# Statistics of a second new batch per group on ScalarE, with a tile of its own for what its passes write

## The chip, the cores and the metric

The kernel runs on one core of a Trainium2 chip. The metric is the device time of one execution in microseconds (us), the median of several runs. The engines are named as in the profile: PE (TensorE), DVE (VectorE), ACT (ScalarE), POOL (GpSimd) and SP (SyncE, which here only issues DMAs).

## The reference

Input `x` is 32 batches of 256 x 1024 (S x N, float32), `adj` is 256 x 256 and serves as the weight of both layers; `b1` and `b2` have 256 elements.

```python
h = jnp.maximum(_layernorm(x, axis=-1), 0.0)      # mean and variance over the 1024 columns of each row
x = x + gnn(h, adj, b1, adj, b2)

def gnn(x, W1, b1, W2, b2):                        # x: (32, 256, 1024)
    adj = construct_adj(x, 8)                      # from the column means: top-9 nodes of an outer product
    xr = jnp.swapaxes(x, 1, 2)
    h = jax.nn.relu(gc(xr, adj, W1, b1))
    h = gc(h, adj, W2, b2)
    return jnp.swapaxes(h, 1, 2)
def gc(x, adj, W, b):                              # degree-normalised adjacency after a linear layer
    return jnp.einsum('bij,bjh->bih', adj / deg, x @ W.T + b)
```

The graph is an outer product of one vector with itself, so its nodes fall into a few classes. The kernel computes the linear layers in full and replaces the product with the 1024 x 1024 graph by sums per class.

## The kernel before

The 32 batches go in 8 groups of 4 (`FIRST[g]` is the first batch of group g). A batch lies in SBUF as 128 partitions x 2 chunks x 1024 columns. 12 slots (`NX`) hold raw batches, 10 slots (`NHL`) the layer-normalised ones, each split in a high and a low float16 part. For each batch:

- Statistics. Either DVE makes them: four `bn_stats` of 128 x 512 (`stats`, L1032 to L1041) and two `bn_aggr` (`mean_var`, L1043); or ACT makes them (`scalar_stats`, L585): a sum pass over each chunk (L594), two small scalings, a square pass over each chunk (L601) and two more small scalings. `on_scalar` (L329) says which: batches 10 and 11, and from 12 on the last batch of each group.
- ACT takes the square root of the variance (`root`, L572), DVE its reciprocal (`root_inverse`, L1051, which counts up `r0_ready`), and POOL makes scale and bias from it in seven small operations (`coefs`, L802 to L820, which begins with a wait for `r0_ready` and ends by counting up `coef_ready`).
- ACT applies them with a relu (`h_chunk`, L614) and writes the high part (`h_hi`, L623); DVE writes the low part (`h_lo`, L1062).
- PE does layer 1 as units of 12 matmuls of 128 x 512 (L430) and adds the graph's part with small matmuls (`rows`, L441). ACT and DVE evict it as a new high and low part (`y_hi` L635, `y_lo` L1071); PE does layer 2 on those, and DVE adds it to `x` (`final`, L1087).

Between these lie the chains of a group. DVE searches the column means for the top nodes (`top_a` to `top_e`, `kinds`) and writes the class mask `onehot[:, g % 2]` (`classes`, L1133). POOL gathers columns of the top nodes (`gather`, L834), DVE sums them (`top_sums`, L1160), and POOL makes the first-layer class input of it (`plain_q1`, L846 and L848). PE multiplies that by the weights (`plain_rows`, L474 with q1r), DVE, ACT, DVE, ACT and DVE turn the result into rows (`rows_x`, `round_rows`, `rows_t`, `round_rest`, `rows_w`). `class_sizes` (L468), `class_q1` (L863 on), `times_q1` (L494) and, for layer 2, `times_q2` (L474 with q) follow the same pattern.

Each engine works through an order written out by hand; a wait holds up everything behind it on its engine. In round g of the main loop (from g = 1) the statistics are those of batches `FIRST[g] + 8` to `FIRST[g] + 11`, and there are such batches in rounds 1 to 5. The orders that matter, in round g:

- POOL (L1006 on): `coefs(first+8)`, `class_sums`, `u_nodes`, `put_u`, `coefs(first+9)`, `late_sums(g)`, the four `gather` of group g+1, **`coefs(first+10)`, `plain_q1(g+1)`, `coefs(first+11)`, `class_q1(g+1)`**.
- ACT (L773 on): `split_rows(2g+1)`, in round 1 the two `make_h` of batch 13, `root(first+10)`, `scalar_stats(first+11)`, `root(first+11)`, `make_h(front(g,3), 0)` (this is batch first+10), `class_count(g+1)`, `split_rows(2g+2)`, `make_h(front(g,3), 1)`, the two of batch first+11.
- DVE (L1433 on): as the loop at L1365 shows.
- PE (L519 on): layer 1 of group g, then layer 2; `plain_rows(g+1)` comes behind `rows(*us[4:6])` of layer 2, then two units, `class_sizes(g+1)` and `rows(*us[6:])`.

What ACT's statistics passes write is not used. It goes into the mask tile `onehot[:, (g + 1) % 2]`, the one that `classes(g+1)` writes next. For that reason `scalar_stats` waits for `l2_ps` (the last readers of that tile) and `classes` for `act_sums` (L1128).

Of the kernel before, what the change touches and what calls it, by code (L numbers as in the profile page):

```python
# [100 lines left out]
def gnn_kernel(nc, x, adj_t, bias1, bias1_row, bias2_row, consts, out):  # L101
# [3 lines left out]
    with ExitStack() as ctx:  # L105
        def sb(name, shape, dt=F32):
            return ctx.enter_context(nc.sbuf_tensor(name, shape, dt))
# [31 lines left out]
        cr = sb("cr", [P, 96], F16)  # L139

        bn = sb("bn", [P, 2, KC, 2, 6])
        mv = sb("mv", [P, RB, KC, 2])
        sums = sb("sums", [P, 2, KC])
        minus = sb("minus", [P, KC])
# [118 lines left out]
        def ends(g):  # L263

            if g < 0:
                return 0
            return FIRST[g] + SIZES[g] if g < NG else B
# [60 lines left out]

        def on_scalar(n):  # L329

            return n in (NX - 2, NX - 1) or n >= NX and n == ends(GROUP[n]) - 1

        def on_scalar_in(g):

            return sum(on_scalar(n) for n in range(min(FIRST[g] + NX, B)))

        def by_vector(n):

# [226 lines left out]
        def _(act):  # L565
# [16 lines left out]
            def scalar_count(n):  # L582
                return n + 1 - by_vector(n)

            def scalar_stats(g, n):  # L585

                if not is_batch(n):
                    return
                done_before, junk = scalar_count(n) - 1, onehot[:, (g + 1) % 2]
                for k in range(KC):  # L590
                    act.wait_ge(x_in[n % NX][k], 16 * (n // NX + 1))
                    if g > 0 and k == 0:
                        act.wait_ge(l2_ps, NH * ends(g - 1))
                    act.activation(junk, xs[:, n % NX, k], ACT.Copy, accum_out=sums[:, 0, k:k + 1]  # L594
                                   ).then_inc(act_sums, 1)
                    act.wait_ge(act_sums, 2 * KC * done_before + k + 1)
                act.activation(mv[:, n % RB, :, 0], sums[:, 0], ACT.Copy, scale=1.0 / N).then_inc(act_means, 1)
                act.activation(minus[:], sums[:, 0], ACT.Copy, scale=-1.0 / N).then_inc(act_means, 1)
                act.wait_ge(act_means, 2 * (done_before + 1))
                for k in range(KC):  # L600
                    act.activation(junk, xs[:, n % NX, k], ACT.Square, bias=minus[:, k:k + 1],  # L601
                                   accum_out=sums[:, 1, k:k + 1]).then_inc(act_sums, 1)
                    act.wait_ge(act_sums, 2 * KC * done_before + KC + k + 1)
                for k in range(KC):
                    act.activation(mv[:, n % RB, k, 1:2], sums[:, 1, k:k + 1], ACT.Copy, scale=1.0 / N
                                   ).then_inc(act_vars, 1)
# [57 lines left out]
            def make_h(n, k):  # L664
                if n is not None:
                    h_chunk(n, k)
                    h_hi(n, k)
# [45 lines left out]
            root(9)  # L713
            means_copy(1, 1)
            make_h(8, 1)
            scalar_stats(0, 10)
            root(10)
            scalar_stats(0, 11)
            root(11)
            make_h(9, 0)  # L720
            make_h(9, 1)
# [6 lines left out]
            for g in range(1, NG):  # L728
# [45 lines left out]
                if g == 1:  # L774
                    n = front(g, 2)
                    make_h(n, 0)
                    make_h(n, 1)
                root(FIRST[g] + 10)
                scalar_stats(g, FIRST[g] + 11)
                root(FIRST[g] + 11)  # L780
                n = front(g, 3)
                make_h(n, 0)
# [248 lines left out]
        def _(dve):  # L1031
# [92 lines left out]

            def classes(g):
                dve.wait_ge(topk, TK * (g + 1))
                if g > 0 and on_scalar_in(g - 1):
                    dve.wait_ge(act_sums, 2 * KC * on_scalar_in(g - 1))  # L1128
                if g == 0:
                    dve.tensor_scalar(onehot[:, 0], kind[:], cs[:, C_WANT:C_WANT + 1], None, ALU.is_equal,  # L1130
                                      ALU.add, accum_out=count[:]).then_inc(onehot_ready, 1)
                else:
                    dve.tensor_scalar(onehot[:, g % 2], kind[:], cs[:, C_WANT:C_WANT + 1], None, ALU.is_equal  # L1133
                                      ).then_inc(onehot_ready, 1)
# [230 lines left out]
            for g in range(1, NG):  # L1365
# [5 lines left out]
                if g == 1:  # L1371
# [21 lines left out]
                    top_c(g + 1)  # L1393
                    top_d(g + 1)
                    root_inverse(first + 9)
                    stats(first + 10, 0)
                    n = front(g, 1)
                    h_lo(n, 0)
                else:
# [14 lines left out]
                    y_lo(*y[3])  # L1414
                    stats(first + 9, 1)
                    mean_var(first + 9)
                    stats(first + 10, 0)
                    root_inverse(first + 9)
                    h_lo(n, 1)
                    y_lo(*y[4])  # L1420
# [11 lines left out]

                end = [u[1:] for u in units(g, 2) + units(g, 3)]  # L1433
                rows_x(2 * g + 1)
                stats(first + 10, 1, (0,))
                rows_t(2 * g + 1)
                stats(first + 10, 1, (1,))
                rows_w(2 * g + 1)
                mean_var(first + 10)
                final(*end[0])  # L1440
                final(*end[1])
                h_lo(n, 1)
                root_inverse(first + 10)
                final(*end[2])
                if to:
                    top_sums(g + 1)
# [2 lines left out]
                if to:  # L1449
                    top_e(g + 1)  # L1450
                    kinds(g + 1)
                    classes(g + 1)
                root_inverse(first + 11)
                if g == 1:
                    n = front(g, 2)
                    h_lo(n, 0)
# [6 lines left out]
                if to:  # L1463
                    class_counts(g + 1)
                    rows_t(2 * (g + 1))
                final(*end[5])
                if to:
                    rows_w(2 * (g + 1))
                if to:
# [30 lines left out]
```

## Time and profile before

| | us |
|---|---|
| median of 3 runs | 495.26 (492.6 to 497.65) |
| the profiled execution | 492.84 |
| its span, first to last instruction | 491.0 |

| engine | busy us | share |
|---|---|---|
| PE | 428.8 | 87% |
| DVE | 399.2 | 81% |
| ACT | 303.2 | 62% |
| POOL | 217.7 | 44% |

The mean granted clock of TensorE was 0.972 of full. The chain of work that ended last is made of DVE for 41%, of PE for 35%, of issue time for 8% and of ACT for 8%. The shares are means over the start, five rounds with new batches to prepare, and two rounds and an end without. In what follows round 3 stands for the steady ones; rounds 2 to 5 repeat it with a period near 52.3 us.

### The profile page before, as it was taken

The numbers are of one execution on the slowest core, as the hardware profiler recorded it, in microseconds if no ns is written. First come the engines' busy times: TensorE is split into PE (matmuls) and PEld (weight loads), VectorE is DVE, ScalarE is ACT, GpSimd is POOL, SyncE is SP. The second block draws the span as 40 slices with busy tenths as digits, with TensorE's granted clock in tenths as the row PEclk, the third lists the DMA queues.
The fourth block names the chain that finished last, engine by engine and source line by source line (L and its number), as shares of the span: only waits on it lengthen the run. The fifth ranks groups of instructions, "written<-read, shape, count | busy, mean of one in ns | idle before, by whom it ended". The sixth has DMA issues, their size and how long they took to land.

```text
span 491.0 us, 7541 instructions
## 1 busy us (share of the span) xinstructions
PE 428.8 (87%) x2220; PEld 177.4 (36%) x2220; DVE 399.2 (81%) x689; ACT 303.2 (62%) x645; POOL 217.7 (44%) x905
## 2 busy tenths in 40 slices
PE   0652799689956999999999999999999999999996
PEld 0111343234322443434443443344343443444332
DVE  4899997897984998999989998999899838763363
ACT  2875487887654777867686677667767734014300
POOL 2445645284607427363537445553736342414200
PEclk9985999999996999999999999999999999999999
DMA  7990000068300648015910683065604310242016
GB/s 293 383 391 11 0 1 1 2 256 280 151 0 1 244 122 320 1 76 224 346 41 3 256 286 144 1 251 184 253 0 159 137 49 1 93 170 83 0 76 267
DMA packets 19402, 68.21 MB, mean 139 GB/s; under 512 B 1825, under 2 KB 2465, under 8 KB 19361
## 3 DMA queue, kind: packets, MB, share of 16 engines
q1 hardware_dynamic: 19360, 67.73, 36.8%
q8 instruction: 18, 0.29, 0.3%
q14 instruction: 24, 0.19, 0.1%
HBM read 34.17 MB, written 33.55 MB: 138 GB/s over the span
## 4 chain that ended last, share of the span: by engine, by line
DVE 41%; PE 35%; issue 8%; ACT 8%; POOL 5%; DMA 1%; POOLq 1%; SPq 0%; DVEq 0%
PE ps L430 28%; DVE hl L1062 9%; DVE hl L1071 8%; DVE xs L1087 6%; DVE bn L1040 6%; PE ps L441 4%; ACT hl L623 3%; ACT hf L614 3%; DVE fv L1103 2%; DVE idx L1111 2%; PE pm L474 1%; DMA xs<-x_dram 1%; POOL nw L816 1%; DVE kind L1097 1%; ACT hl L635 1%
## 5 line engine op out<-in xcount | busy, mean ns | idle before, releaser
L430 PE MATMUL ps<-hl,wh 128*128 128x512 f16 x1024 | 308.3, 383 | 21.2 <-DVE wl L1244 11.3
L430 PE MATMUL ps<-hl,wl 128*128 128x512 f16 x512 | 195.5, 382 | 0.0
L430 PEld LDWEIGHTS ps<-hl,wh 128*128 128x128 f16 x1024 | 95.2, 99 | 152.7 <-issue 38.0
L1071 DVE SCALAR_TENSOR_TENSOR hl<-ps,hl 128x1024 f16<-128x1024 f32 (+1 forms) x73 | 76.2, 1087 | 30.4 <-ACT hl L635 30.4
L635 ACT ACTIVATE hl<-ps 128x512 f16<-128x512 f32 x128 | 74.4, 595 | 40.9 <-PE ps L441 40.9
L614 ACT ACTIVATE hf<-xs,nbias,rstd 128x1024 f32<-128x1024 f32 x64 | 79.1, 1236 | 17.6 <-POOL nbias L820 12.5
L1087 DVE SCALAR_TENSOR_TENSOR xs<-ps,sc,xs 128x1024 f32<-128x1024 f32 (+1 forms) x71 | 78.8, 1139 | 11.5 <-PE ps L441 11.5
L1062 DVE TENSOR_TENSOR hl<-hf,hl 128x1024 f16<-128x1024 f32 x64 | 76.9, 1213 | 12.2 <-ACT hl L623 12.0
L430 PEld LDWEIGHTS ps<-hl,wl 128*128 128x128 f16 x512 | 50.5, 99 | 61.6 <-issue 1.9
L1040 DVE BATCH_NORM_STATS2 bn<-xs 128x6 f32<-128x512 f32 x100 | 63.7, 678 | 6.6 <-DMA xs<-x_dram 6.5
L623 ACT ACTIVATE hl<-hf 128x1024 f16<-128x1024 f32 x64 | 67.6, 1056 | 2.0
L834 POOL COPY gat<-hl 128x4 f16 x256 | 44.6, 226 | 23.8 <-DVE idx L1111 15.2
L810 POOL TENSOR_TENSOR nw<-r 128x2 f32<-128x2 f32 x32 | 7.1, 223 | 98.5 <-DVE r L1055 98.2
L441 PE MATMUL ps<-onehot,lw 32*128 32x512 bf16 x256 | 39.8, 379 | 4.9 <-DVE lw L1185 4.9
L649 ACT ACTIVATE ra<-rx 128x256 bf16<-128x256 f32 x16 | 6.7, 416 | 41.1 <-DVE rx L1174 33.7
L579 ACT ACTIVATE std<-mv,eps 128x2 f32<-128x2 f32 x32 | 9.4, 294 | 30.4 <-DVE mv L1048 30.1
L635 ACT ACTIVATION_READ_ACCUMULATOR hl<-ps 128x1 f32 x128 | 26.4, 206 | 0.0
L403 PE MATMUL pm<-hl,ones_h 128*32 128x512 f16 x16 | 7.8, 513 | 18.1 <-ACT hl L623 15.6
L863 POOL TENSOR_TENSOR q<-s_t,rdeg 128x16 f32<-128x16 f32 x8 | 5.6, 706 | 30.6 <-issue 30.6
L441 PEld LDWEIGHTS ps<-onehot,lw 32*128 32x128 bf16 x256 | 7.4, 92 | 31.7 <-issue 23.5
L662 ACT ACTIVATE kind<-onehot 128x1024 f16<-128x1024 bf16 x7 | 7.4, 1054 | 15.3 <-DVE onehot L1133 15.3
L601 ACT ACTIVATE onehot<-xs,minus 128x1024 bf16<-128x1024 f32 x14 | 16.1, 1148 | 0.5
(138 smaller groups left out, 447.1 us busy)
## 6 DMA issues: line engine op xcount, KB each, us to landing
xs<-x_dram SPq DMA_DIRECT2D x62, 512.0 KB, 7.6
out_dram<-xs SPq DMA_DIRECT2D x31, 1024.0 KB, 5.1
xs<-x_dram SPq DMA_DIRECT2D x4, 256.0 KB, 3.3
out_dram<-xs SPq DMA_DIRECT2D x4, 256.0 KB, 2.1
wt<-adj_t_dram SPq DMA_DIRECT2D x1, 256.0 KB, 9.6
b1r<-b_row_dram SPq DMA_DIRECT2D x1, 128.0 KB, 9.4
b2r<-b_row_dram SPq DMA_DIRECT2D x1, 128.0 KB, 11.4
cs<-consts_dram SPq DMA_DIRECT2D x1, 84.5 KB, 9.4
```

The source lines that it names most:

```text
L430: pe.matmul(bank(i, m), w[:, k, o], hl[:, slot, part, k, cols], start=(k == 0 and w is wh and part == 0), stop=False)
L441: last = pe.matmul(bank(place(layer, n, half), m), lw[at, layer - 1, m * P:(m + 1) * P], onehot[at, g % 2, half * HALF:(half + 1) * HALF], ...
L601: act.activation(junk, xs[:, n % NX, k], ACT.Square, bias=minus[:, k:k + 1], accum_out=sums[:, 1, k:k + 1]).then_inc(act_sums, 1)
L614: act.activation(hf[:, c % NHF], xs[:, n % NX, k], ACT.Relu, bias=nbias[:, n % RB, k:k + 1], scale=rstd[:, n % RB, k:k + 1], accum_out=s_a ...
L623: act.activation(hl[:, n % NHL, 0, k], hf[:, c % NHF], ACT.Copy).then_inc(hi_ready, 1)
L635: last = act.activation(hl[:, n % NHL, 0, m, half * HALF:(half + 1) * HALF], bank(i, m), ACT.Relu, accum_out=acc[:, g % 2, half, m, LANE[n ...
L834: pool.tensor_copy(gat[:, j, t], hl[:, slot, :, :, bass.ds(v, 1)].rearrange("p a k o -> p a (k o)")).then_inc(gathered, 1)
L1040: dve.bn_stats(bn[:, n % 2, k, half], xs[:, n % NX, k, half * HALF:(half + 1) * HALF]).then_inc(stats_done, 1)
L1062: dve.tensor_tensor(hl[:, n % NHL, 1, k], hf[:, c % NHF], hl[:, n % NHL, 0, k], ALU.subtract).then_inc(lo_ready, 1)
L1071: last = dve.scalar_tensor_tensor(hl[:, n % NHL, 1, ms, cols], banks(i, piece), 0.0, hl[:, n % NHL, 0, ms, cols], ALU.max, ALU.subtract)
L1087: last = dve.scalar_tensor_tensor(xs[:, n % NX, ms, cols], banks(i, piece), scal(S_C2), xs[:, n % NX, ms, cols], ALU.mult, ALU.add)
L1103: dve.match_replace(fv[:], top[:, 0], fv[:], -1e-30).then_inc(topk, 1)
```

## The change

`scalar_stats` now also makes the statistics of batch first+10 in each round: batches 14, 18, 22, 26 and 30, beside 15, 19, 23, 27 and 31. DVE's `stats` and `mean_var` for them go. ACT's passes write to a tile `junk` of their own, so that `scalar_stats` no longer waits for `l2_ps`, and `classes` waits for `l2_ps` of two groups before in place of `act_sums`. On DVE `root_inverse(first+10)` moves to where `root_inverse(first+11)` was, behind `classes(g+1)`, and `root_inverse(first+11)` moves behind `final(*end[5])`. POOL's and PE's orders stay.

```diff
+        junk = sb("junk", [P, N], BF16)
...
         def on_scalar(n):
 
-            return n in (NX - 2, NX - 1) or n >= NX and n == ends(GROUP[n]) - 1
-
-        def on_scalar_in(g):
-
-            return sum(on_scalar(n) for n in range(min(FIRST[g] + NX, B)))
+            return n in (NX - 2, NX - 1) or n >= NX and n >= ends(GROUP[n]) - 2
...
-            def scalar_stats(g, n):
+            def scalar_stats(n):
...
-                done_before, junk = scalar_count(n) - 1, onehot[:, (g + 1) % 2]
+                done_before = scalar_count(n) - 1
                 for k in range(KC):
                     act.wait_ge(x_in[n % NX][k], 16 * (n // NX + 1))
-                    if g > 0 and k == 0:
-                        act.wait_ge(l2_ps, NH * ends(g - 1))
-                    act.activation(junk, xs[:, n % NX, k], ACT.Copy, accum_out=sums[:, 0, k:k + 1]
+                    act.activation(junk[:], xs[:, n % NX, k], ACT.Copy, accum_out=sums[:, 0, k:k + 1]
...
+                scalar_stats(FIRST[g] + 10)
                 root(FIRST[g] + 10)
-                scalar_stats(g, FIRST[g] + 11)
+                scalar_stats(FIRST[g] + 11)
                 root(FIRST[g] + 11)
...
             def classes(g):
                 dve.wait_ge(topk, TK * (g + 1))
-                if g > 0 and on_scalar_in(g - 1):
-                    dve.wait_ge(act_sums, 2 * KC * on_scalar_in(g - 1))
+                if g > 1:
+                    dve.wait_ge(l2_ps, NH * ends(g - 2))
...
                     root_inverse(first + 9)
-                    stats(first + 10, 0)
                     n = front(g, 1)
...
                     mean_var(first + 9)
-                    stats(first + 10, 0)
                     root_inverse(first + 9)
...
                 rows_x(2 * g + 1)
-                stats(first + 10, 1, (0,))
                 rows_t(2 * g + 1)
-                stats(first + 10, 1, (1,))
                 rows_w(2 * g + 1)
-                mean_var(first + 10)
                 final(*end[0])
                 final(*end[1])
                 h_lo(n, 1)
-                root_inverse(first + 10)
                 final(*end[2])
...
                     classes(g + 1)
-                root_inverse(first + 11)
+                root_inverse(first + 10)
...
                 final(*end[5])
+                root_inverse(first + 11)
                 if to:
                     rows_w(2 * (g + 1))
```

## Rows read from the trace of the kernel before

**Rows 1.** The page, part 1: busy time, share of the span, instructions.
```profile
PE 428.8 (87%) x2220; PEld 177.4 (36%) x2220; DVE 399.2 (81%) x689; ACT 303.2 (62%) x645; POOL 217.7 (44%) x905
```

**Rows 2.** PE timeline (start, us, engine, line, op, [idle before]): times_q2, one means.
```profile
247.88 1.05 PE L461 MATMUL pm<-hl,ones_h 128*32 128x512 f16 x16
...
260.34 0.28 PE L474 MATMUL pm<-wh,q 128*128 128x256 f16 x1 [0.19 <-POOL q L979]
...
417.29 0.28 PE L474 MATMUL pm<-wh,q 128*128 128x256 f16 x1 [0.30 <-POOL q L979]
...
466.77 0.28 PE L474 MATMUL pm<-wh,q 128*128 128x256 f16 x1 [0.30 <-POOL q L979]
```

**Rows 3.** Timeline of PE, round 3: rows, plain_rows(4), class_sizes(4).
```profile
264.47 0.60 PE L441 MATMUL ps<-onehot,lw 32*128 32x512 bf16 x4 [0.71 <-DVE lw L1185]
...
274.21 0.28 PE L474 MATMUL pm<-wh,q1r 128*128 128x256 f16 x1
...
280.05 0.21 PE L468 MATMUL pm<-cr,ones_h 128*128 128x96 f16 x1
```

**Rows 4.** Timeline of DVE, round 3, around what the change takes out.
```profile
246.54 1.23 DVE L1040 BATCH_NORM_STATS2 bn<-xs 128x6 f32<-128x512 f32 x2
...
249.29 1.22 DVE L1062 TENSOR_TENSOR hl<-hf,hl 128x1024 f16<-128x1024 f32 x1 [1.46 <-ACT hl L623]
...
262.02 0.42 DVE L1174 SCALAR_TENSOR_TENSOR rx<-pm,b2r 128x256 f32<-128x256 f32 x1
262.35 0.69 DVE L1040 BATCH_NORM_STATS2 bn<-xs 128x6 f32<-128x512 f32 x1
262.95 0.47 DVE L1178 SCALAR_TENSOR_TENSOR rt<-ra,cs,rx 128x256 f32<-128x256 bf16 x1
...
265.11 2.48 DVE L1087 SCALAR_TENSOR_TENSOR xs<-ps,sc,xs 128x1024 f32<-128x1024 f32 x2 [0.49 <-PE ps L441]
```

**Rows 5.** Timeline of ACT: two statistics of the start, then round 3.
```profile
90.60 1.04 ACT L594 ACTIVATE onehot<-xs 128x1024 bf16<-128x1024 f32 x1
...
102.10 1.23 ACT L614 ACTIVATE hf<-xs,nbias,rstd 128x1024 f32<-128x1024 f32 x1
...
246.66 0.29 ACT L579 ACTIVATE std<-mv,eps 128x2 f32<-128x2 f32 x1 [2.32 <-DVE mv L1048]
...
263.46 0.42 ACT L653 ACTIVATE rb<-rt 128x256 bf16<-128x256 f32 x1 [0.57 <-DVE rt L1178]
...
271.41 1.24 ACT L614 ACTIVATE hf<-xs,nbias,rstd 128x1024 f32<-128x1024 f32 x1 [0.71 <-POOL nbias L820]
```

**Rows 6.** Timeline of DVE, round 3: the reciprocal behind classes(4).
```profile
274.73 0.16 DVE L1055 RECIPROCAL r<-std 128x2 f32<-128x2 f32 x1
```

**Rows 7.** Timeline of POOL, round 3: coefs(22) begins, plain_q1(4) ends, coefs(23) begins.
```profile
269.64 0.19 POOL L810 TENSOR_TENSOR nw<-r 128x2 f32<-128x2 f32 x1
...
271.68 0.31 POOL L848 TENSOR_TENSOR q1r<-s_t,q1r 128x24 f16<-128x24 f32 x1
...
274.97 0.20 POOL L810 TENSOR_TENSOR nw<-r 128x2 f32<-128x2 f32 x1 [2.98 <-DVE r L1055]
```

**Rows 8.** Timeline of POOL, round 1: coefs(15), first and last operation.
```profile
168.00 1.09 POOL L810 TENSOR_TENSOR nw<-r 128x2 f32<-128x2 f32 x1 [3.63 <-DVE r L1055]
...
171.30 0.20 POOL L820 TENSOR_TENSOR nbias<-nw,rstd 128x2 f32<-128x2 f32 x1
```

**Rows 9.** Timeline of PE, round 1: plain_rows(2).
```profile
167.37 0.28 PE L474 MATMUL pm<-wh,q1r 128*128 128x256 f16 x1
```

**Rows 10.** Timeline of DVE, end of round 1: h_lo(14, 1).
```profile
176.29 1.23 DVE L1062 TENSOR_TENSOR hl<-hf,hl 128x1024 f16<-128x1024 f32 x1 [0.65 <-ACT hl L623]
```

**Rows 11.** Windows: us, busy of PE, PEld, DVE, ACT, POOL, PEclk, DMA, GB/s.
```profile
92.00:97.00 5.00, 1.18 (x6) 0.41 (x5) 4.92 (x8) 4.84 (x12) 0.41 (x2) 1.00 0.00 2
144.00:148.00 4.00, 0.00 (x0) 0.00 (x0) 3.96 (x8) 0.00 (x0) 1.75 (x5) 0.77 0.00 0
152.00:158.00 6.00, 6.00 (x22) 2.49 (x22) 2.60 (x8) 3.46 (x6) 4.58 (x32) 0.63 0.00 0
```

More of the change, by code:

```diff
@@ L600, in scalar_stats @@
                 for k in range(KC):
-                    act.activation(junk, xs[:, n % NX, k], ACT.Square, bias=minus[:, k:k + 1],
+                    act.activation(junk[:], xs[:, n % NX, k], ACT.Square, bias=minus[:, k:k + 1],
                                    accum_out=sums[:, 1, k:k + 1]).then_inc(act_sums, 1)
@@ L715, in _ @@
             make_h(8, 1)
-            scalar_stats(0, 10)
+            scalar_stats(10)
             root(10)
-            scalar_stats(0, 11)
+            scalar_stats(11)
             root(11)
```

## The prediction

> **What bounds the kernel now.** I read the page's part 1 first: PE is busy 87% and DVE 81% of the span, ACT 62%, POOL 44% [rows 1]. That makes PE or DVE the bound and says ACT has room, but it is a mean over unlike stages. So I went to the timeline of one steady round and asked where each engine waits. From round 3 to round 6 the same PE work, `times_q2`, recurs every (417.29 - 260.34) / 3 = 52.32 us; from 6 to 7, where DVE has few statistics and searches left and PE also leaves out two sets of column means (16 matmuls, 1.05 us each), it is 49.48 us [rows 2]. With the means back that is 51.5 to 51.6 us: what PE alone needs. A round with full DVE work thus holds only some 0.8 us that a lighter DVE could give back. PE and DVE are in near balance, and the small waits go to and fro: PE waits 0.71 us for DVE's `rows_w` [rows 3], DVE 0.49 us for PE and 1.46 us for ACT [rows 4].
>
> **What the change removes.** Per round, on DVE: two `bn_stats` (1.23 us) before `h_lo`, two more between the steps of the rows, and two `bn_aggr` of some 0.35 us together; about 2.8 us, 14 us over five rounds. I cost each by what stands behind it:
> - The first two run from 246.54 to 247.7. The next large DVE instruction is `h_lo` at 249.29, after a wait of 1.46 us for ACT's high part [rows 4]. ACT made that behind its own `root(21)`, which waited 2.32 us for DVE's `mean_var(21)` and started at 246.66 [rows 5]. `mean_var(21)` comes ahead of the removed pair, so ACT gets no earlier, and the wait grows from 1.46 to 2.7 us. Saved on the path: 0. Without that cover it would be 1.2 us a round.
> - The other two fill the time in which ACT rounds a row tile: `rows_x` starts at 262.02, `bn_stats` at 262.35, `rows_t` at 262.95 [rows 4], and 0.42 us of ACT lie between plus the way there and back. The next pair repeats it. Saved: 0 to 0.1 us.
> - `mean_var(22)` is followed by `final`, which waits 0.49 us for PE [rows 4]. Saved: 0; the wait grows.
> - The wait of `classes` on ACT's sums costs nothing now, since DVE shows no idle time there; its new one, on matmuls of two groups back, costs nothing either. The own tile is needed, though: ACT's second statistics end near 275.3 (below), after `classes(4)` at 274.33.
>
> So hardly any of the 14 us reaches the path.
>
> **What it adds to ACT.** Two statistics with their roots took 102.10 - 90.60 = 11.50 us, 5.75 us each [rows 5]. In round 3 ACT can begin them as soon as it has issued `round_rest` at 263.46, near 263.8 [rows 5]: batch 22 is through with its root near 269.5 and batch 23 near 275.3. The batches have been loaded long before: DVE read batch 22 at 246.54.
>
> **What it moves.** This is the step that I take to decide. `root_inverse(22)` now stands where `root_inverse(23)` stood, at 274.73 [rows 6], less 0.1 us for the reciprocal that is gone from before. Its input is there from 269.5. It counts up `r0_ready`, and POOL's `coefs(22)` waits for that; behind `coefs(22)` in POOL's order stands `plain_q1(4)`, and for that waits PE's `plain_rows(4)`. Before, `coefs(22)` began at 269.64 and `plain_q1(4)` had ended at 271.99 [rows 7], 2.2 us before PE came to it at 274.21 without a wait [rows 3]. After: reciprocal 274.65, `coefs(22)` 0.24 us later as in round 3 now (274.73 to 274.97) at 274.9, `plain_q1` ends 2.35 us on (271.99 - 269.64), 277.25, PE starts at 277.3. **PE stands still for 277.3 - 274.2 = 3.1 us.**
>
> Does anything take it back? Behind it on PE lie two units and `class_sizes(4)`, 280.05 - 274.21 = 5.84 us later [rows 3]: 283.15. DVE's `rows_x(8)` waits for PE too, until about 278.2. ACT's `make_h(22, 0)` starts at 276.7, when POOL's bias is there, not at 271.41 [rows 5]; with 2.4 us for it, 1.06 for `class_count` and 0.4 for the rounding, DVE's `rows_w(8)` ends near 282.7, in time for PE. `class_degrees(4)` waits for `class_sizes`, so DVE's next `h_lo` comes at 284.1 in place of 280.99. `coefs(23)` ends near 284.3, `class_q1(4)` near 287.4, and PE wants it at 289.7. So DVE and PE both leave the round 3.1 us late, in the phase in which they stood before, and round 4 repeats it. Rounds 2 to 5: 4 x 3.1 = 12.4 us.
>
> Round 1 differs. ACT makes batch 13 first, and while POOL does `coefs`, DVE runs two `h_lo` (they begin 0.1 us behind the reciprocal). `coefs(15)`, which stood at this place, took from 168.00 to 171.50 [rows 8], and `coefs(14)` now takes its place with the same neighbours: I take its 3.5 us, not the 1.75 us of other places. `plain_q1(2)` follows, 0.62 us, and PE starts at 172.2 instead of 167.37 [rows 9]: 4.8 us of idle PE. PE is not the bound just there: DVE is led by ACT's `make_h(14, 1)` and by `rows_t`, and `h_lo(14, 1)` comes near 178.7 in place of 176.29 [rows 10], 2.4 us late; PE catches up in its waits for DVE that follow (about 3 us in round 2). Round 1: 2.4 us, between 2 and 4.8.
>
> The Trainium skill, GPSIMD Engine Reference, section Specifications, says that GpSimd shares its SBUF interface with VectorE and is held up by VectorE instructions with two SBUF inputs. By that rule `coefs(14)` is stretched, as the row shows for `coefs(15)`; with the plain 1.75 us the stall would be 3.1 us there too, and the sum about the same.
>
> **The sum.** 12.4 + 2.4 = 14.8 us, less 0 to 0.5 of small savings, so 14.7. The profiled execution has a span of 491.0 us and took 492.84 us; it becomes 505.7 and 507.5 us. The median of the runs lies 2.4 us above it, so I predict 510 us.
>
> **Rivals.**
> - *The clock falls in the new stalls.* In the wait of round 1, in which PE did nothing from 144 to 148 and on to 152, the granted clock left 1.00 for 0.5 (1.2 GHz): 0.77 is the mean of the first window, and 0.63 that from 152 to 158, so 4.4 us at half rate after the restart, 2.2 us lost. From 92 to 97 PE was busy for 1.18 us of 5.00, a stall of 3.8 us, and the clock stayed at 1.00 (2.4 GHz) [rows 11]. Stalls of 3.1 us should leave it alone, that of 4.8 us may not. If it fell in all five: 510 + 11 = 521; in two or three, 515. Chance of two or more: 0.17. The Trainium skill, TensorE: Matmul & The Clock Gate, section Part 1, says that the low clock is the resting state and that activity releases it; by that, each new stall is a candidate. The trace agrees for the long wait of round 1 and not for 3.8 us.
> - *ACT becomes the bound.* If its waits did not swallow the addition, 5 x 5.75 = 28.8 us, 524 us. Against it: its batch 23 is done at 275.3 and it then still waits 1.4 us for POOL. Chance 0.05.
> - *The stall is covered.* If the removed 2.8 us did move DVE's search forward, the reciprocal would come at 271.9 and PE would wait 0.3 us: five rounds give 1 to 2 us, 496 to 497, no change. For it: DVE is busy nearly all the time from 265.11 to 274.73. Against it: each removed piece lies ahead of a wait. With only the first pair (1.2 us) getting through, 5 x 1.9, minus little, is 9 us: 504. Chance of no change: 0.10.
> - *Faster: DVE's relief reaches PE.* It takes the whole 2.8 us and more: only if the reciprocal of batch 22 comes more than 3.1 us earlier than computed here does PE not wait at all, and then each steady round gives at most 0.8 us, 4 x 0.8 = 3.2 us, plus up to 4 us in round 1, where DVE's lead over PE's waits is larger: 488 to 492 us. Chance 0.05.
>
> The forecast itself has 0.63. About 1% (5 us) is what a measurement of this kernel can tell from no change. Faster by more: 0.05; within: 0.10; slower: 0.85. The range must leave out no more than 2 in 10: from below the case with one pair getting through (502) to the clock falling in most stalls (519).
>
> **What would show each step.** Right: PE idle before `plain_rows` (L474 with q1r), released by POOL, about 3 us in rounds 2 to 5 and near 5 in round 1; POOL idle before `coefs(first+10)` for `r0`, from the last gather on; DVE idle before `rows_x` of the even rows; DVE's wait for ACT before `h_lo` grown to 2.7 us; a period near 55.4 us; rounds 6 and 7 as before. Wrong: PE's new wait under 1 us (DVE came sooner), or a wait of DVE or POOL for ACT's root of batch first+10 (ACT is the bound), or a clock under 0.95.

## The result, and the profile after

| | before | after |
|---|---|---|
| median of the runs | 495.01 us (492.6 to 497.65, 4 runs) | 517.38 us (514.9 to 519.87, 4 runs) |
| profiled execution, its span | 492.84 us, 491.0 us | 519.87 us, 518.0 us |
| granted clock, mean of each run | 0.972 (profiled) | 0.941 (profiled), 0.953, 0.947, 0.937 |

The changed kernel takes 1.0464 times as long, 95% interval 1.0423 to 1.0505: 22.4 us more by the medians (21 to 25 by the interval). 510 (502 to 519) was forecast, so the sign and the range held, and the forecast was 7.4 us short.

The page after, part 1 (busy time, share of the span, instructions), answers to [rows 1]:

```profile
PE 442.6 (85%) x2220; PEld 181.5 (35%) x2220; DVE 388.1 (75%) x654; ACT 329.4 (64%) x705; POOL 209.1 (40%) x905
```

DVE lost 11.1 us and ACT gained 26.2 us of work, as the diff says. The number to look at is PE's: the same 2220 matmuls are busy 13.8 us longer. No work was added to PE, so they ran slower: that is the clock.

PE's waits (released by, us in total, times, longest). The first line has no counterpart before the change. The second has (9.0 us, 4 times): most of it is the long wait of round 1, in both kernels.

```profile
PE pm L471 <- POOL q1r L844: 16.5, 5, 4.7
...
PE pm L471 <- POOL q L975: 9.4, 6, 8.0
```

The timeline of PE after, up to three lines per round (start, us, engine, line, operation, idle time before it): `times_q2` (q), `plain_rows` (q1r) and `class_sizes` (cr). The first 271.41 answers to the 260.34 of [rows 2], and 288.25 and 295.79 to 274.21 and 280.05 of [rows 3].

```profile
175.52 0.39 PE L471 MATMUL pm<-wh,q1r 128*128 128x256 f16 x1 [4.66 <-POOL q1r L844]
...
183.72 0.21 PE L465 MATMUL pm<-cr,ones_h 128*128 128x96 f16 x1
...
233.08 0.28 PE L471 MATMUL pm<-wh,q1r 128*128 128x256 f16 x1 [2.90 <-POOL q1r L844]
...
238.92 0.21 PE L465 MATMUL pm<-cr,ones_h 128*128 128x96 f16 x1
...
271.41 0.28 PE L471 MATMUL pm<-wh,q 128*128 128x256 f16 x1 [0.27 <-POOL q L975]
...
288.25 0.28 PE L471 MATMUL pm<-wh,q1r 128*128 128x256 f16 x1 [3.03 <-POOL q1r L844]
...
295.79 0.21 PE L465 MATMUL pm<-cr,ones_h 128*128 128x96 f16 x1
...
345.18 0.39 PE L471 MATMUL pm<-wh,q1r 128*128 128x256 f16 x1 [3.02 <-POOL q1r L844]
...
353.88 0.21 PE L465 MATMUL pm<-cr,ones_h 128*128 128x96 f16 x1
...
386.37 0.28 PE L471 MATMUL pm<-wh,q 128*128 128x256 f16 x1 [0.28 <-POOL q L975]
...
403.11 0.39 PE L471 MATMUL pm<-wh,q1r 128*128 128x256 f16 x1 [2.90 <-POOL q1r L844]
...
411.86 0.21 PE L465 MATMUL pm<-cr,ones_h 128*128 128x96 f16 x1
...
444.35 0.28 PE L471 MATMUL pm<-wh,q 128*128 128x256 f16 x1 [0.28 <-POOL q L975]
```

Two things are to be read here. First the stalls: 4.66, 2.90, 3.03, 3.02 and 2.90 us, where 4.8 and four times 3.1 were computed. Then what comes behind each: from `plain_rows` to `class_sizes` it was 5.84 us before ([rows 3]); now it is 8.20, 5.84, 7.54, 8.70 and 8.75 us. The matmuls between them are the same, and none of them waits, so 2.35 + 0 + 1.7 + 2.86 + 2.9 = 9.8 us were lost behind four of the five stalls.

The windows of two of them (us, busy of PE, PEld, DVE, ACT, POOL, PEclk, DMA, GB/s), stall and what follows:

```profile
284.60:288.20 3.60, 0.63 (x5) 0.11 (x4) 2.29 (x5) 2.27 (x6) 1.84 (x9) 1.00 1.04 366
288.20:296.20 8.00, 7.95 (x35) 3.49 (x35) 4.13 (x9) 6.82 (x11) 1.47 (x7) 0.79 0.23 88
341.60:345.10 3.50, 0.56 (x5) 0.06 (x4) 2.22 (x5) 2.18 (x6) 1.82 (x9) 0.87 1.02 364
345.10:354.10 9.00, 8.92 (x33) 3.90 (x35) 3.87 (x8) 7.79 (x13) 1.49 (x8) 0.67 0.23 87
```

The granted clock is below 1.00 (2.4 GHz) while PE is busy throughout: part of each stretch was granted 0.5 (1.2 GHz). A mean of 0.79 over 8 us is (1 - 0.79) x 8 = 1.7 us of full speed lost, 0.67 over 9 us is 3.0 us. Both agree with the times above.

The chain behind the stall at 288.25, from the timelines of DVE, POOL and ACT. DVE first; 285.62 answers to 274.73 of [rows 6]:

```profile
285.22 0.49 DVE L1129 TENSOR_SCALAR onehot<-kind,cs 128x1024 bf16<-128x1024 f16 x1
285.62 0.16 DVE L1051 RECIPROCAL r<-std 128x2 f32<-128x2 f32 x1
...
289.12 0.42 DVE L1168 TENSOR_TENSOR rx<-pm,b1r 128x256 f32<-128x256 f32 x1 [2.16 <-PE pm L471]
```

POOL; it answers to 269.64 and 271.68 of [rows 7]:

```profile
285.86 0.19 POOL L806 TENSOR_TENSOR nw<-r 128x2 f32<-128x2 f32 x1 [5.23 <-DVE r L1051]
...
287.90 0.30 POOL L844 TENSOR_TENSOR q1r<-s_t,q1r 128x24 f16<-128x24 f32 x1
```

ACT, the bias that it waits for instead (0.71 in [rows 5]):

```profile
287.62 1.24 ACT L609 ACTIVATE hf<-xs,nbias,rstd 128x1024 f32<-128x1024 f32 x1 [1.26 <-POOL nbias L816]
```

Here `classes` ends, the reciprocal follows, POOL has sat idle for 5.23 us waiting for it, does `coefs`, then `plain_q1`, and PE starts. Reciprocal to PE's restart: 2.63 us, where 2.65 was computed.

### The profile page after: what moved, and what is told of

It reads as the page before. It is cut to its first block, busy times and chain, and to the rows that moved or that the text cites. A ratio compares the mean times of both kernels' runs of the same rounds, so it can differ in the third digit from the quotient of the medians.

```text
span 518.0 us, 7565 instructions
## 1 busy us (share of the span) xinstructions
PE 442.6 (85%) x2220; PEld 181.5 (35%) x2220; DVE 388.1 (75%) x654; ACT 329.4 (64%) x705; POOL 209.1 (40%) x905
## 4 chain that ended last, share of the span: by engine, by line
PE 40%; DVE 36%; issue 8%; POOL 7%; ACT 6%; DMA 1%; POOLq 1%; SPq 0%; DVEq 0%
PE ps L427 32%; DVE hl L1067 8%; DVE hl L1058 7%; DVE xs L1083 5%; DVE bn L1036 5%; PE ps L438 4%; ACT hl L618 2%; PE pm L471 2%; DVE fv L1099 2%; ACT hf L609 2%; DVE idx L1107 2%; DMA xs<-x_dram 1%; DVE kind L1093 1%; ACT hl L630 1%; POOL nw L812 1%
## 5 line engine op out<-in xcount | busy, mean ns | idle before, releaser
L427 PE MATMUL ps<-hl,wh 128*128 128x512 f16 x1024 | 317.8, 393 | 19.1 <-DVE wl L1240 11.3
L427 PE MATMUL ps<-hl,wl 128*128 128x512 f16 x512 | 199.8, 390 | 0.0
L427 PEld LDWEIGHTS ps<-hl,wh 128*128 128x128 f16 x1024 | 97.6, 101 | 155.7 <-issue 48.1
L427 PEld LDWEIGHTS ps<-hl,wl 128*128 128x128 f16 x512 | 51.5, 101 | 65.0 <-issue 8.1
L806 POOL TENSOR_TENSOR nw<-r 128x2 f32<-128x2 f32 x32 | 8.8, 275 | 131.9 <-DVE r L1051 131.6
L1036 DVE BATCH_NORM_STATS2 bn<-xs 128x6 f32<-128x512 f32 x80 | 50.7, 679 | 6.1 <-DMA xs<-x_dram 6.1
L596 ACT ACTIVATE junk<-xs,minus 128x1024 bf16<-128x1024 f32 x24 | 27.6, 1148 | 0.8
L589 ACT ACTIVATE junk<-xs 128x1024 bf16<-128x1024 f32 x24 | 25.2, 1049 | 0.4
L471 PE MATMUL pm<-wh,q1r 128*128 128x256 f16 x32 | 8.5, 327 | 16.5 <-POOL q1r L844 16.5
```

The costliest lines, as they stand in the source:

```text
L427: pe.matmul(bank(i, m), w[:, k, o], hl[:, slot, part, k, cols], start=(k == 0 and w is wh and part == 0), stop=False)
L589: act.activation(junk[:], xs[:, n % NX, k], ACT.Copy, accum_out=sums[:, 0, k:k + 1]).then_inc(act_sums, 1)
L596: act.activation(junk[:], xs[:, n % NX, k], ACT.Square, bias=minus[:, k:k + 1], accum_out=sums[:, 1, k:k + 1]).then_inc(act_sums, 1)
L1036: dve.bn_stats(bn[:, n % 2, k, half], xs[:, n % NX, k, half * HALF:(half + 1) * HALF]).then_inc(stats_done, 1)
```

## Experiments

All ratios are to runs of the kernel before on the same chip, with 95% intervals.

**e3_recip_moved_only: of the parts of the change, which one costs?** The kernel before, with nothing but its two reciprocals in their new places; DVE keeps its statistics, ACT gets none.

```
                 h_lo(n, 1)
-                root_inverse(first + 10)
                 final(*end[2])
...
                     classes(g + 1)
-                root_inverse(first + 11)
+                root_inverse(first + 10)
...
                 final(*end[5])
+                root_inverse(first + 11)
```

> The kernel before with only the two reciprocals moved to where the changed kernel has them; DVE keeps the statistics of batch first+10 and ACT makes none of them. Queue theory: the whole loss is there, the same waits of PE for POOL (3 us in rounds 2 to 5, 4.7 in round 1) and the same falls of the clock: 517 us (514 to 520). Rival, that ACT's added 28 us carry a part of the loss: clearly less, 505 us. Rival, that DVE's relief had given something back: more than the changed kernel, by up to 3 us.

Measured: 519.11 us (518.3 to 519.57) against 495.12, ratio 1.0486, 1.0448 to 1.0523. PE's waits in it:

```profile
PE pm L474 <- POOL q1r L848: 16.6, 5, 4.7
```

Two instructions of 0.16 us, of which the first comes one search later (268.63 before, 285.62 in the round above, whose other rows stand 11 us later), are enough for the whole loss: the same five waits with the same sum as in the changed kernel, and behind the same four of them `class_sizes` comes late (8.14, 5.85, 7.53, 8.58 and 8.65 us after `plain_rows`). Its 519.11 us and the changed kernel's 517.38 can't be told apart: the intervals of the two ratios overlap.

**e1_pool_order: is it the order of POOL's queue?** The changed kernel, with `plain_q1` ahead of `coefs` on POOL.

```
-                coefs(first + 10)
                 if is_group(g + 1):
                     plain_q1(g + 1)
+                coefs(first + 10)
```

> The changed kernel with one edit on POOL: plain_q1(g+1) stands ahead of coefs(first+10), so that plain_q1 no longer waits for the reciprocal of batch first+10; the reciprocals stay late. Queue theory (PE's new stall comes from plain_q1 queued behind coefs): PE's wait of 3 us before plain_rows for POOL is gone in all five rounds. But batch first+10 still gets its bias late (5 us), so ACT's make_h, class_count and the rounding behind it are late, and PE should wait about 2.6 us for rows_w before the last rows of the round: 5 x 2.6 = 13 us over before, 508 us, or up to 515 if the clock falls in these waits too. Rival, that the wait for POOL is the whole cost: 495 to 497 us. Rival, that ACT's added work is the bound: as slow as the changed kernel, 517 us, with no PE wait moved.

Measured: 507.05 us (505.8 to 508.61), ratio 1.0245, 1.0204 to 1.0287. PE has no wait for `q1r` any more, so the order of the queue was the stall's mechanism. But only 10.3 of the 22.4 us come back, as expected (508 us). The rest moved on; two lines show where, the first of DVE, the second of PE (1.46 in [rows 4], 0.71 in [rows 3]):

```profile
256.94 1.22 DVE L1058 TENSOR_TENSOR hl<-hf,hl 128x1024 f16<-128x1024 f32 x1 [2.15 <-ACT hl L618]
```

```profile
272.07 0.60 PE L438 MATMUL ps<-onehot,lw 32*128 32x512 bf16 x4 [1.03 <-DVE lw L1181]
```

The same row stands at 217.12 one round earlier: a period of 54.95 us, with PE now waiting in small pieces (PE's waits for DVE's `xs` grew from 4.6 us in all to 7.5, for `cr` from 2.4 to 6.0, for `lw` from 4.9 to 6.8). What stands behind them is what was expected, the bias of batch 22, which is still late. ACT:

```profile
284.28 1.24 ACT L609 ACTIVATE hf<-xs,nbias,rstd 128x1024 f32<-128x1024 f32 x1 [1.28 <-POOL nbias L816]
```

This `make_h(22, 0)` starts 2.5 us behind `plain_rows(4)` (281.81); before, it started 2.8 us ahead of it (271.41 and 274.21, [rows 5] and [rows 3]). ACT had both statistics done 1.28 us earlier and waited, so the late reciprocal ends last here and not ACT's load. The load fills that wait without adding to it: in e3, which has none of it, ACT waits 5.97 us for the same bias.

**e2_recip_early: the reciprocal ahead of the search.** The changed kernel; ACT keeps both statistics.

```
                 final(*end[3])
+                root_inverse(first + 10)
                 if to:
                     top_e(g + 1)
                     kinds(g + 1)
                     classes(g + 1)
-                root_inverse(first + 10)
```

> The changed kernel with one edit on DVE: root_inverse(first+10) stands ahead of top_e(g+1) instead of behind classes(g+1), about 3.3 us earlier; ACT still makes both statistics. Queue theory: coefs and plain_q1 are done before PE gets to plain_rows, the wait for POOL goes. What is left is ACT: it is free for make_h of batch first+10 near 275.3 in the time of round 3 of before, 4 us later than before, and rows_w comes some 1.2 us after PE wants it: 5 x 1.2 = 6 us over before, 501 us (499 to 505), clock near 0.97. Rival, ACT as the bound of the changed kernel: 510 us or more. Rival, the late reciprocal as the whole cost: 495 us.

Measured: 502.76 us (501.58 to 503.69), ratio 1.0156, 1.0117 to 1.0194. That is within what was expected. The stall before `plain_rows` is 0.74 to 0.87 us in rounds 2 to 5 and 1.92 us in round 1, where it was expected to go. POOL's timeline says why:

```profile
277.80 0.20 POOL L806 TENSOR_TENSOR nw<-r 128x2 f32<-128x2 f32 x1 [2.02 <-DVE r L1051]
...
279.06 1.19 POOL L814 TENSOR_TENSOR rstd<-nw,r 128x2 f32<-128x2 f32 x1
...
280.83 0.35 POOL L844 TENSOR_TENSOR q1r<-s_t,q1r 128x24 f16<-128x24 f32 x1
```

One operation on 128x2 took 1.19 us in place of 0.20: 1.0 us beside a DVE instruction on 128x1024 (278.97 to 280.20), as the prediction had seen in `coefs(15)` [rows 8]. That is more than the 0.86 us that PE waited. Here ACT goes from its second statistics to `make_h(22, 0)` without a wait, so this is where its load ends last: the period is 53.8 us, 1.5 over before, and PE's wait for POOL is in it.

**e4_fill: how much is idle time, how much the clock?** The changed kernel, with dummy matmuls in PE's stall, so that it is busy while it waits and starts its real work no later.

```
             def plain_rows(g):
+                if 2 <= g < NG - 1:
+                    pe.wait_ge(row_x, 2 * g)
+                    pe.wait_ge(fv_copied, NH * (g + 1))
+                    for _ in range(FILL[g]):
+                        pe.matmul(pm_r, ones_h[:], wh[:, 0], start=True, stop=True)
                 pe.wait_ge(q1r_ready, 2 * (g + 1))
...
+            FILL = {2: 40, 3: 26, 4: 26, 5: 26, 6: 26}
```

> The changed kernel with matmuls of 128 columns by 256 put in front of PE's wait for plain_q1, 26 in rounds 2 to 5 (some 2.9 us) and 40 in round 1 (4.4 us); their result is overwritten and not used. Waits and orders stay. Clock theory (of the loss of 22.4 us about 15 are the idle time itself, the rest is half clock after it): PE's clock stays at 1.00 after the stalls, mean near 0.965, and the time is 510 us (508 to 512). Rival, that the 7 us beyond the sum come from something else (waits further on that grow): 517 us with a higher clock.

Measured: 507.2 us (505.27 to 508.63), ratio 1.0244, 1.02 to 1.0289. `times_q2` in its trace, rounds 3 and 4, and a window that holds the filled stall:

```profile
264.26 0.28 PE L471 MATMUL pm<-wh,q 128*128 128x256 f16 x1 [0.28 <-POOL q L981]
...
319.43 0.28 PE L471 MATMUL pm<-wh,q 128*128 128x256 f16 x1 [0.28 <-POOL q L981]
```

```profile
278.00:287.00 9.00, 8.91 (x59) 5.41 (x57) 5.72 (x12) 7.00 (x15) 2.55 (x12) 1.00 0.54 201
```

The clock stays at 1.00, the period is 55.17 us (then 55.20 and 55.12), 2.85 us over the 52.32 of before, and 10.2 us of the changed kernel's time are gone though PE's real work waits as long for POOL. So 22.4 us are 12.2 us of delay (9.9 to 14.3 by the interval) and 10.2 us of clock, the latter uncertain by some 3 us by the two intervals. The rival of 517, that the clock costs nothing, falls.

**e5_dve_relief_only: is DVE's relief worth anything?** The kernel before; the four `bn_stats` of batches 14, 18 and so on are left out, so that their scale comes from stale statistics. ACT gets no work for it.

```
             def stats(n, k, halves=(0, 1)):
-                if n is None or not is_batch(n):
+                if n is None or not is_batch(n) or left_out(n):
```

> The kernel before without the four bn_stats of batches 14, 18, 22, 26 and 30; nobody makes them, bn_aggr reads what earlier batches left, so the result of these batches is not the reference's. All else, the reciprocals too, stands as before. It measures DVE's relief alone, 2.5 us a round, 12.3 in all. Theory (each removed piece lies ahead of a wait): DVE's wait for ACT before h_lo grows from 1.46 to 2.7 us, time 494 to 495.5 us, no change. Rival, that the relief reaches PE: 0.8 us a round and up to 4 in round 1, 488 to 492 us.

Measured: 494.60 us (490.16 to 496.92, 12 runs) against 494.59 (23 runs), ratio 0.9995, 0.9966 to 1.0023. One line of DVE, the counterpart of 249.29 in [rows 4]:

```profile
253.16 1.23 DVE L1065 TENSOR_TENSOR hl<-hf,hl 128x1024 f16<-128x1024 f32 x1 [2.14 <-ACT hl L623]
```

The wait for ACT took up what was removed: 1.46 us became 2.14, with 0.36 more before the reciprocal. Some 12 us of DVE's work are gone (20 `bn_stats` of 0.6 us), and between 1.7 us gained and 1.1 us lost is all that the interval leaves. The two `bn_aggr` a round, the other part of the relief, stayed.

**e6_act_load_only: what does ACT's new work cost by itself?** The kernel before, DVE unchanged; ACT makes the statistics of batch `first + 10` a second time, into tiles that nobody reads.

```
                 root(FIRST[g] + 10)
+                extra_stats(FIRST[g] + 10, g - 1)
                 scalar_stats(g, FIRST[g] + 11)
```

> The kernel before with the statistics of batch first+10 made a second time, by ACT, behind root(first+10) and ahead of scalar_stats(first+11), into tiles that nobody reads; DVE keeps its own, the reciprocals stay. It measures ACT's added 5.75 us a round alone. Theory: ACT comes to make_h of batch first+10 4.7 us later, rows_w about 2 us after PE wants it: 8 to 10 us over before, 504 us (501 to 507). Rival, ACT has room for all of it: 495 to 496 us. Rival, ACT is the bound: 520 us.

Measured: 507.24 us (506.0 to 507.74) against 494.59, ratio 1.0259, 1.0211 to 1.0307: a little above what was expected. That is 12.6 us. PE's waits name DVE's `xs`, 4.6 us in all before:

```profile
PE ps L435 <- DVE xs L1113: 11.6, 7, 3.8
```

It is an upper bound for what the same load costs in the changed kernel. Here it stands behind `root(first + 10)`, which waits 0.77 us for DVE's `mean_var`: ACT begins it 1.40 us after the start of `round_rest` (272.53 to 273.93), in e1 0.32 us after it (271.08 to 271.40). That is 1.1 us a round, so 5 of the 12.6 us by estimate; e2, with the load in the change's own place and the reciprocal early, loses 7.6 us. Neither adds to the loss of the change: in the changed kernel and in e1 ACT's work is done before the late bias comes, and e3, without it, is no faster.

**e7_split_passes: the same work in ACT's own wait.** All of the change's work is moved to ACT, but its two passes for the sums run ahead of `split_rows(2g + 1)`, where ACT waits for DVE's rows, and the reciprocals stay where they were before.

```
+                scalar_stats(FIRST[g] + 10, (0,))
                 split_rows(2 * g + 1)
...
+                scalar_stats(FIRST[g] + 10, (1,))
                 root(FIRST[g] + 10)
```

> The changed kernel with the sum passes of batch first+10 moved into ACT's wait ahead of split_rows(2g+1), the square passes where they are, and both reciprocals where the kernel before has them. Theory: ACT does 2.6 us of its added 5.75 in a wait of 3 us, is ready for make_h of batch first+10 only 1 us later than before, and class_count behind it still waits for the mask: no wait of PE for POOL, clock near 0.97, time 493 to 496 us, equal to before or a little less. Rival, that the relief of DVE is worth something once nothing is late: 489 to 492 us. Rival, that ACT's load costs wherever it lies: 500 us or more.

Measured: 495.99 us (492.4 to 497.74, 12 runs), ratio 1.0035, 1.0007 to 1.0062; periods of 52.14, 52.34 and 52.38 us. Both costs are gone but for 0.3 to 3.1 us, and nothing is gained: the balance of DVE against ACT is not what sets the time.

**e8_pool_before: the same pattern, already in the kernel before.** [rows 11] has PE doing nothing from 144 to 148 in round 1. PE waits 8.22 us there for `late_sums(1)` of POOL, which stands behind `coefs(13)` in POOL's order; and that waits 10.99 us for its reciprocal. The kernel before, with `coefs(13)` behind `late_sums(1)`:

```
-                coefs(first + 9)
+                if g > 1:
+                    coefs(first + 9)
                 put_u(first + 2)
                 put_u(first + 3)
                 late_sums(g)
+                if g == 1:
+                    coefs(first + 9)
```

> The kernel before with one edit on POOL, in round 1 only: coefs(13) stands behind late_sums(1), not ahead of the last two put_u, so that the input of times_q2(1) no longer waits for the reciprocal of batch 13. It is the pattern that the change brought in, at the one place where before already has it: PE waits 8.2 us there for POOL, and the clock falls. Theory: PE's wait before times_q2 of round 1 shrinks to under 1 us; DVE then sets the pace (rows_x(3) near 148.2 in place of 153.5), the fall of the clock there goes: 5 to 8 us less than before, 487 to 490 us. Rival, the wait comes back elsewhere (DVE's search, ACT): under 2 us gained.

Measured: 487.98 us (486.25 to 490.87, 6 runs) against 494.54 (18 runs), ratio 0.9886, 0.9835 to 0.9938. It has the lowest median of the study, below both kernels of the case. Its POOL and then its PE in round 1:

```profile
142.81 0.69 POOL L979 TENSOR_TENSOR q<-p,q 128x96 f16<-128x96 f32 x2
146.48 0.19 POOL L810 TENSOR_TENSOR nw<-r 128x2 f32<-128x2 f32 x1 [2.98 <-DVE r L1058]
```

```profile
144.08 0.27 PE L474 MATMUL pm<-wh,q 128*128 128x256 f16 x1
...
151.08 1.03 PE L441 MATMUL ps<-onehot,lw 32*128 32x512 bf16 x4 [3.60 <-DVE lw L1188]
```

`times_q2` starts at 144.08 without a wait, at 151.98 before. 8.2 us of wait are gone and 3.6 us have come back as a wait for DVE's rows, which is late next. That makes 4.6 us, and the two profiled executions differ by 4.1; the medians differ by 6.6 (3.1 to 8.2 by the interval). One part of the expectation failed: the clock still falls there, to 0.50 from 150 to 156, behind the wait of 3.60 us.

**e9_pool_split: e7 and e8 together.** Does DVE's relief shorten that next wait?

> The kernel with the split passes and the reciprocals in their old places (ACT makes both statistics), with the same edit on POOL in round 1. Theory: the same 5 to 8 us under its own parent, and since DVE now sets the pace in round 1, the statistics that DVE no longer makes there (1.2 us ahead of rows_x) should give about 1 us back: 487 to 490 us, level with or 1 us better than the kernel before with that edit. Rival: DVE's relief is worth nothing here either, 1 to 2 us slower than that one.

Measured: 488.95 us (488.49 to 489.9), ratio 0.9898, 0.9855 to 0.994. The wait is shorter, 2.37 in place of 3.60 us, but 0.64, 0.26 and 0.87 us follow elsewhere, and behind it too the clock falls, to 0.54 from 152 to 154. No better than e8 alone.

**e10_swap_split and e11_swap_before: does removing the wait behind which the relief vanishes set it free?** In rounds 2 and on, ACT makes its high part ahead of `root(first + 9)`, and DVE takes `h_lo` ahead of that reciprocal. e10 does it to e9, with DVE relieved; e11 to e8, with DVE's full work.

```
-                    root(FIRST[g] + 9)
                     make_h(n, 1)
+                    root(FIRST[g] + 9)
...
-                    root_inverse(first + 9)
                     h_lo(n, 1)
+                    root_inverse(first + 9)
```

> The kernel of the run before this, and from round 2 on make_h(n, 1) stands ahead of root(first+9) on ACT, and on DVE root_inverse(first+9) behind h_lo(n, 1). It takes away the wait that swallowed DVE's relief: h_lo no longer waits for ACT, which waited for DVE's mean_var. Theory: DVE reaches rows_x about 1 us earlier in rounds 2 to 5, and PE's need of 51.5 us a round is the limit: up to 0.8 us a round, 2 to 3 us less, 484 to 487 us, period of rounds 3 to 5 near 51.6. Rival, another wait (column means, ACT's evictions) holds the pace: no change.

> The kernel before with the edit on POOL and with the same swap on ACT and DVE; DVE keeps the statistics of batch first+10, 1.2 us of them right before that h_lo. Against the run before this it shows what DVE's relief is worth once its cover is gone. Theory: part of the gain of the swap is used up by the statistics, 1 to 2 us slower than the one with the relief: 486 to 489 us. Rival: PE is the bound in both, same time.

Measured: e10 489.35 us (486.39 to 491.31, 10 runs), ratio 0.9893, 0.9862 to 0.9925; e11 489.6 us (486.71 to 491.58, 9 runs), ratio 0.9904, 0.9869 to 0.9938. Both missed their ranges, and neither is faster than e8 or e9. `h_lo` no longer waits and PE's wait for `lw` is gone, and the relief is still worth nothing. e10's trace shows what came in its place. ACT, POOL, PE, then DVE:

```profile
251.81 0.60 ACT L638 ACTIVATE hl<-ps 128x512 f16<-128x512 f32 x1 [1.58 <-PE ps L438]
```

```profile
254.46 0.20 POOL L961 TENSOR_TENSOR ka<-acc 128x8 f32<-128x8 f32 x1 [5.45 <-ACT hl L638]
...
256.61 1.67 POOL L984 TENSOR_TENSOR q<-p,q 128x96 f16<-128x96 f32 x2
```

```profile
258.34 0.28 PE L471 MATMUL pm<-wh,q 128*128 128x256 f16 x1 [1.27 <-POOL q L984]
```

```profile
256.75 1.31 DVE L1070 TENSOR_TENSOR hl<-hf,hl 128x1024 f16<-128x1024 f32 x1
```

PE's last products release ACT at 251.81, ACT's fourth sum releases POOL at 254.46, and POOL releases PE at 258.34. It is a way from PE to PE over two other engines, and PE has less work to put into it than it takes. The next `times_q2` of e10 is at 310.75: 52.41 us, no shorter than the 52.32 of before. But DVE has a hand in it. The last step on POOL, two operations, takes 1.67 us where e8 has 0.69 (255.51 in its trace): `h_lo`, which e8 starts at 256.80, behind `times_q2` (256.25), now comes ahead of `times_q2` and runs beside that step. In the last of these rounds, where no `h_lo` lies there, the pair takes 0.69 us again, PE waits 0.28 us in place of 1.27, and the interval to it is 51.42 us (363.15 to 414.57). e11 shows the same (1.67 us, a wait of 1.27 us, then 51.41 us). So 1.0 of the 1.27 us is a collision that the swap itself brought in; what the relief is worth without that, no run shows.

## Why the prediction was right, and where it fell short

The mechanism that was forecast is the one that the runs show. The number, 517.4 us, lies near what the prediction gave for its first rival with the clock falling four times (510 + 4 x 2.2 = 518.8 us) and not near its centre; the range held because it took most of that rival in, though the rival had a chance of 0.17. Of the signs of being wrong that it names, one came true: a clock under 0.95 (0.941, 0.947 and 0.937 in three of four executions).

- **The moved reciprocal decides.** Right, and e3 shows it alone. The stalls of rounds 2 to 5 measured 2.90 to 3.03 us, not 3.1; the period without the clock's part grew by 2.85 us, to 55.17 us (e4), where 55.4 was forecast; with the clock's part it is 56.86 to 58.10 us. "Rounds 2 to 5: 4 x 3.1 = 12.4 us" measured 11.4.
- **Round 1.** "4.8 us of idle PE" was 4.66, and of this 2.5 us stayed at the round's end (in e4, from `times_q2` of round 1 to the first rows of round 2: 150.47 to 213.22, 62.75 us, in place of 60.27). 2.4 was computed. The stretched `coefs(14)` took 3.5 us, as taken from [rows 8]. The price by bounds from the nearest row held.
- **The sum.** Without the clock: 11.4 + 2.5 = 13.9 by the periods, 12.2 by the medians, where 14.7 was forecast. These 0.8 to 2.5 us too many made up for a part of the clock that was left out.
- **The clock is the mis-sized term.** "Stalls of 3.1 us should leave it alone, that of 4.8 us may not" failed. It fell behind four of five, for 9.8 us in the trace and 10.2 us by e4. Its price had been worked out well (2.2 us each, 1.7 to 2.9 measured), its chance had not: 0.17 for two or more. The step rested on one stall of 3.8 us in one execution of one kernel. The same stall, in the same place and ahead of anything that the change moves, looks otherwise in the trace after. First two windows of it, then the second of them before (its first is in [rows 11]):

```profile
92.00:97.00 5.00, 1.18 (x6) 0.31 (x4) 4.91 (x8) 4.84 (x13) 0.77 (x2) 0.80 0.01 2
97.00:103.00 6.00, 6.00 (x18) 2.12 (x16) 4.30 (x6) 5.80 (x15) 5.48 (x31) 0.60 0.54 212
```

```profile
97.00:103.00 6.00, 6.00 (x30) 2.46 (x29) 6.00 (x8) 5.81 (x14) 5.50 (x28) 1.00 0.48 188
```

  The same wait, the same 1.18 us of work beside it, and one execution kept 2.4 GHz where the other fell. In e4 and e7 it was kept; in e1, e2, e3 and e6 it fell. So [rows 11] showed one throw of a die, and not that such a stall is safe. The Trainium skill, TensorE: Matmul & The Clock Gate, section Part 1, warns that the number of slow matmuls differs from run to run of one kernel. The executions of the kernel before agree (mean granted clocks from 0.958 to 0.976), and the prediction should have let that widen the chance.
- **The profiled execution.** Its span grew by 27.0 us: 13.9 of delay (taken from e4), 9.8 of clock behind the new stalls, and 3.4 that were lost before any moved instruction ran, as `times_q2` of round 1 starts at 155.39 in place of 151.98. The windows above show part of that loss. Together that is 27.1. The medians differ by less, 22.4 us: the profiled execution after is the slowest of its four, the one before lies near its fastest (492.84 in 492.6 to 497.65 us). That the kernel before loses such pieces of clock too in slower executions is not shown by a trace of its own; e5, whose instructions are the same up to there, shows it in an execution of 496.92 us (0.72 from 97 to 103, `times_q2` of round 1 at 155.70).
- **DVE's relief.** "So hardly any of the 14 us reaches the path": e5 measures 0 (-1.1 to +1.7 us). The wait of 1.46 us was to grow to 2.7; it is 0.36 + 2.15 in the trace after:

```profile
257.97 0.17 DVE L1051 RECIPROCAL r<-std 128x2 f32<-128x2 f32 x1 [0.36 <-ACT std L576]
...
260.28 1.23 DVE L1058 TENSOR_TENSOR hl<-hf,hl 128x1024 f16<-128x1024 f32 x1 [2.15 <-ACT hl L618]
```

- **ACT isn't the bound.** True of the changed kernel (its wait for POOL's bias is 1.26 us, 1.4 was computed), and of e1. But the wait that takes up ACT's added work is made by the late reciprocal: 5.97 us in e3, 1.26 with the load. Where the reciprocal comes early (e2) or in its old place (e6), the load costs up to 7.6 and up to 12.6 us. The chance of 0.05 was right for the change as it stands; of the room that ACT has once the reciprocal is in time it says nothing.
- **The cap of 0.8 us a round** was put down to what a lighter DVE could give back. In e10 and e11 PE no longer waits for DVE's rows in the steady rounds, and the period stays at 52.4 us: 1.27 us of wait came back on the way PE, ACT, POOL, PE, most of it POOL's step beside `h_lo`. Where that is missing the interval is 51.4 us, so the cap itself (51.5 to 51.6 us of PE's need) was about right. It did no harm, since that rival had 0.05.

Left open: which stall lets the clock fall. 2.90 us kept it once (233.08) and lost it once (403.11) in one trace, 2.37 us lost it in e9, and no run here was made to find out what separates them.

## What to carry to other kernels

Before moving a small instruction, follow its semaphore to the queue of the engine that waits for it, and ask what stands behind that wait: here 0.16 us on DVE, released later, held up a ready `plain_q1` on POOL and with it PE, five times. Look for the same pattern in the kernel as it is: an instruction that waits ahead of one that is ready cost 8.2 us in round 1, and putting the waiting one behind gained 6.6 us (e8), more than any work that was taken off an engine. When a stall has been taken away, ask what its lateness had covered, and what the instructions that now come earlier will run beside (e10). And price each new stall of PE with the clock that may fall behind it (here some 2 us for each 3), with a chance drawn from several executions, not from one.

## What the runs showed of the hardware

- The granted clock went from 1.00 (2.4 GHz) to 0.5 (1.2 GHz) behind stalls of 2.90, 3.02, 3.03 and 4.66 us in which PE did nothing (e9: 2.37 us, e8: 3.60 us), and not behind another of 2.90 us; a stall of 3.8 us kept it in some executions and lost it in others. Each fall behind the change's stalls cost 1.7 to 2.9 us of PE's time.
- Dummy matmuls in the wait kept the clock (1.00 in the window of e4) and saved 10.2 us of 517.4, though nothing uses what they compute.
- A POOL operation on 128x2, 0.19 to 0.20 us elsewhere, took 1.19 us beside a DVE instruction on 128x1024 (e2), and a pair on 128x96, 0.69 us in e8, took 1.67 us beside DVE's `h_lo` (e10): 1.0 us more each time. In e2 that is more than the 0.86 us that PE waited, in e10 most of the 1.27 us.
